# A four-layer cross-attention kernel: q turned by transfers from group 2 on, fused layer-norm rows, and another order in the first pass

## The reference

```
L0: xn = layer_norm(x); q, k, v from xn and context with weights quantised to {-g, 0, g}
    x = x + softmax(q k^T / sqrt(8)) v Wo           16 heads of 8
L1: self-attention, cross-attention (16 heads of 8, masks), feed-forward of 512 with gelu,
    each with residual and layer_norm
L2: vision = mean of context; three steps of routing weights; fused = text + gate * weighted
    out = layer_norm(fused) * gamma + beta
L3: h = rmsnorm(x); q = h Wq (16 heads of 64), k, v = rmsnorm(context) Wk, Wv (4 heads of 64)
    q = q*cos + rotate_half(q)*sin;  k = k*cos + rotate_half(k)*sin
    x = x + softmax(q k^T / 8 + mask) v Wo;  x = x + (silu(h Wgate) * (h Wup)) Wdown
```

## Time and profile before

| | |
|---|---|
| Median of 3 runs | 474.1 us (473.9 to 476.17) |
| The profiled execution | 470.89 us |
| Its span | 469.0 us |
| PE busy | 433.0 us, 92% |
| DVE busy | 372.8 us, 79% |
| ACT busy | 298.4 us, 64% |
| POOL busy | 285.2 us, 61% |

### The profile page before, as it was taken

One profiled execution on the slowest core, in us unless ns is written; L12 is line 12 of the kernel. 1 busy time (PEld: TensorE's weight loads), 2 busy tenths in 40 slices (PEclk: granted clock), 3 DMA queues, 4 the chain that ended last, 5 costly groups with the idle time before them and its releaser, 6 DMA issues.

```text
span 469.0 us, 16877 instructions
## 1 busy us (share of the span) xinstructions
PE 433.0 (92%) x6824; PEld 348.2 (74%) x6824; DVE 372.8 (79%) x927; ACT 298.4 (64%) x726; POOL 285.2 (61%) x323
## 2 busy tenths in 40 slices
PE   5899999999999999999888888989999999989896
PEld 4467777766767777689877666888888888878676
DVE  5598898689999898877788987869788686868553
ACT  1478777678787776766873656566575757654452
POOL 6565733357878787965553666558566666753430
PEclk9999999999999999999999999999999999999999
DMA  8990000000000000000000000000000000000000
GB/s 275 235 288 13 3 2 3 2 3 3 1 4 3 1 4 3 2 1 2 1 1 3 2 1 3 1 13 3 14 3 1 14 3 13 1 14 1 15 1 24
DMA packets 12436, 11.54 MB, mean 25 GB/s; under 512 B 5192, under 2 KB 10312, under 8 KB 12360
## 3 DMA queue, kind: packets, MB, share of 16 engines
q1 hardware_dynamic: 11640, 9.01, 7.4%
q10 hardware_dynamic: 720, 1.45, 0.9%
HBM read 9.42 MB, written 1.05 MB: 22 GB/s over the span
## 4 chain that ended last, share of the span: by engine, by line
PE 50%; DVE 24%; ACT 10%; issue 8%; POOL 7%; DMA 1%; POOLq 0%; ACTq 0%; DVEq 0%
PE ps L471 9%; PE ps L485 6%; PE ps L453 6%; POOL p L1929 4%; PE ps L461 3%; PE ps L639 3%; ACT shared L864 2%; PE ps L411 2%; PE ps L537 2%; PE ps L412 2%; PE ps L501 2%; ACT p L858 2%; PE ps L420 2%; DVE sm L1654 2%; DVE wide L1564 2%
## 5 line engine op out<-in xcount | busy, mean ns | idle before, releaser
L1346 DVE TENSOR_REDUCE negm<-ps 128x8 bf16<-128x512 f32 x96 | 59.6, 683 | 20.8 <-PE ps L453 20.8
L1879 POOL TENSOR_TENSOR wide<-wide,cv 128x1024 f32<-128x1024 f32 x24 | 45.6, 1899 | 44.3 <-ACT wide L848 44.3
L858 ACT ACTIVATE p<-ps 128x512 f32<-128x512 f32 x96 | 57.1, 598 | 23.4 <-PE ps L461 21.9
L864 ACT ACTIVATE shared<-ps 128x512 f32<-128x512 f32 x96 | 55.1, 604 | 20.1 <-PE ps L471 20.1
L471 PE MATMUL ps<-cst,p 128*128 128x128 f32 x384 | 61.2, 282 | 2.6 <-ACT p L858 0.6
L471 PEld LDWEIGHTS ps<-cst,p 128*128 128x128 f32 x384 | 42.2, 141 | 26.0 <-ACT p L858 15.1
L1822 POOL TENSOR_TENSOR rstd<-veps,neghalf 128x2 f32<-128x2 f32 x40 | 28.9, 721 | 41.9 <-DVE veps L1382 23.8
L1929 POOL TENSOR_TENSOR p<-p,mx 128x512 f32<-128x512 f32 x32 | 33.9, 1060 | 29.0 <-DVE mx L1650 28.7
L1936 POOL TENSOR_TENSOR probs<-p,rc 128x512 f32<-128x512 f32 x32 | 33.4, 1054 | 7.9 <-DVE rc L1657 7.8
L1059 ACT ACTIVATE p<-p 128x512 f32<-128x512 f32 x32 | 20.1, 631 | 21.5 <-POOL p L1929 21.5
L461 PE MATMUL ps<-negm,idb 128*128 128x512 bf16 x96 | 32.8, 382 | 0.4 <-DVE negm L1346 0.4
(11 more groups left out here) (214 smaller groups left out, 1131.3 us busy)
## 6 DMA issues: line engine op xcount, KB each, us to landing
m<-in_mask_l SPq DMA_DIRECT2D x2, 512.0 KB, 12.8
result<-x_all SPq DMA_DIRECT2D x7, 128.0 KB, 1.8
x_all<-in_x_tok SPq DMA_DIRECT2D x1, 768.0 KB, 7.0
wide<-in_ctx_t SPq DMA_DIRECT2D x1, 768.0 KB, 8.5
rv<-in_rv ACTq DMA_DIRECT2D x1, 768.0 KB, 8.4
wa<-in_wa SPq DMA_DIRECT2D x1, 512.0 KB, 9.0
w<-in_w SPq DMA_DIRECT2D x2, 256.0 KB, 7.5
wq<-in_wq SPq DMA_DIRECT2D x1, 512.0 KB, 7.7
```

The lines of the kernel that those rows point to most:

```text
L858: A_(p3[:, n % 3, :], ps[:, S_BANK[r], :], ACT.Exp, scale=SC8).then_inc(sm["act_exp"], 1)
L864: A_(pt[:, w % 2, r, :], pt_bank(RG * w + r), ACT.Copy).then_inc(sm["act_pt"], 1)
L1346: V.tensor_reduce(negm[:, n % 4, :], ps[:, S_BANK[r], :].rearrange("p (a k) -> p a k", k=S), AX.X, ALU.max, negate=True).then_inc(sm["dve_ ...
L1879: P.tensor_tensor(r_op[:, w % 2, :, :], k_t[:, w % 2, :].unsqueeze(1).to_broadcast([128, 4, GT]), head_masks.unsqueeze(2).to_broadcast([12 ...
```

## The change

**q turned in full (groups 2 to 7).** VectorE makes q*(-sin) into `q_sin` (in `shared`) with `sine`, and q*cos into `q_rows` with `read_q`: eight operations of 128x512 a group in place of four of 128x1024. SyncE copies `q_sin` to `q_swap` with the halves of 32 partitions exchanged: for each pair of q tiles four transfers of 32 partitions x 4 KB. GpSimd adds `q_swap` to `q_rows` (`turn_q`, four operations of 128x512). The scores are one product with `kt`; `kcs` and the fill `ks` are gone for these groups. The mask is added by VectorE as before.

**Order of the last stage.** q2 and q3 are filled at the end of the first half. VectorE makes q0, q1 at the end of its first half and q2, q3 at the head of its second; `rotate_k` stands ahead of `out`. GpSimd's `turn_q` are in its second half, two between the subtracts and two at the end. ScalarE reads `l_in` ahead of `exps3`.

**Fused rows.** `l2_norm` and `l2_affine` are replaced by `l2_rows` in all rounds.

**Pass 0.** `x` comes in three pieces; the loads that ScalarE issued (`rv`, `cst`) are issued by SyncE; ScalarE normalises groups 0 and 1 and makes two of unit 0's four masked keys; the quantisation's scales take three operations in place of four; unit 1's transposes and projections stand inside unit 0 of TensorE's loop, and ScalarE reads them after unit 0's first exponential.

```diff
         HALVES = (
             (("s0", 0), ("s1", 0), ("pv0", -1), ("pv1", -1), ("l_in", 2), ("md", -2), ("l_text", 2), ("k", 2), ("out", -1),
-             ("in", 1), ("l_gate", 2), ("t0", 0), ("t1", 0), ("q0", 1), ("q1", 1)),
-            (("s0", 0), ("s1", 0), ("pv0", -1), ("pv1", -1), ("m_in", -1), ("kt", 2), ("ks", 2), ("q2", 1), ("q3", 1),
-             ("out", -1), ("v", 2), ("mg0", -1), ("mu0", -1), ("l_back", 2), ("t0", 0), ("mg1", -1), ("mu1", -1), ("t1", 0)),
+             ("in", 1), ("l_gate", 2), ("q0", 1), ("q1", 1), ("t0", 0), ("t1", 0), ("q2", 1), ("q3", 1)),
+            (("s0", 0), ("s1", 0), ("pv0", -1), ("pv1", -1), ("m_in", -1), ("kt", 2),
+             ("v", 2), ("out", -1), ("mg0", -1), ("mu0", -1), ("l_back", 2), ("t0", 0), ("mg1", -1), ("mu1", -1), ("t1", 0)),
         )
...
+            def swap_halves(g):
+                half = HD3 // 2
+                for a in range(2):
+                    eng.wait_ge(sm["q_sin"], 4 * (g - TURNED) + 2 * a + 2)
+                    if g > TURNED:
+                        eng.wait_ge(sm["q_rot"], 4 * (g - TURNED - 1) + 2 * a + 2)
+                    two = slice(2 * a, 2 * a + 2)
+                    for i in range(4):
+                        to, of = half * i, half * (i ^ 1)
+                        eng.dma_start(q_swap[to:to + half, two, :], q_sin[of:of + half, two, :])\
+                           .then_inc(sm[f"q_swap{a}"], 16)
...
+            normalise_in(0)
+            act.wait_ge(sm["ld_small"], 32)
+            A_(idb[:, 0, :], cst[:, 0:128], ACT.Copy).then_inc(sm["cst_bf"], 1)
             evac_in(0)
             evac_qk(0)
+            mask_half()
+            normalise_in(1)
             evac_in(1)
-            evac_qk(1)
...
                 exps(w, 0)
+                if w == 0:
+                    evac_qk(1)
                 exps(w, 1)
...
+            def q_times(g, i, to, c):
+                tab = cst[:, C_ROPEQ + c * S:C_ROPEQ + c * S + S].unsqueeze(1).to_broadcast([128, 2 * GB, S])
+                return V.tensor_tensor(to, bank_of(f"q{i}", g).rearrange("p (b q) -> p b q", q=S), tab, ALU.mult)
...
@@ VectorE, first_half(r)
                 if r < NG - 1:
-                    l2_norm(r + 1)
+                    l2_rows(r + 1)
                 read("mg1", r - 2)
                 read("mu1", r - 2)
...
                     sum3(2 * n + 1)
+                if r + 2 < NG:
+                    rotate_k(r + 2)
                 if 1 <= r < NG:
                     read("out", n - 1)
                     m_rms_mean(r - 1)
                 if r + 2 < NG:
                     l2_max(r + 2)
+                if r + 1 < NG:
+                    sine(r + 1, 0)
+                    read("q0", r + 1)
+                    read("q1", r + 1)
                 if r + 2 < NG:
-                    rotate_k(r + 2)
                     l2_gate(r + 2)
...
@@ GpSimd
+            def turn_q(g, i):
+                pool.wait_ge(sm[f"q_swap{i // 2}"], 64 * (g - TURNED + 1))
+                pool.wait_ge(*released(f"q{i}", g))
+                P.tensor_tensor(q_rows(g, i), q_rows(g, i), q_swap[:, i, :].rearrange("p (b q) -> p b q", q=S), ALU.add)\
+                    .then_inc(sm["q_rot"], 1)
...
@@ GpSimd, second_half(r)
+                if r + 1 < NG:
+                    turn_q(r + 1, 0)
                 if r < NG:
                     subtract3(4 * r + 2)
+                if r + 1 < NG:
+                    turn_q(r + 1, 1)
+                if r < NG:
                     subtract3(4 * r + 3)
                 if r + 2 < NG:
                     l2_fuse(r + 2)
                 if r < NG:
                     probs3(4 * r + 2)
                     probs3(4 * r + 3)
+                if r + 1 < NG:
+                    turn_q(r + 1, 2)
+                    turn_q(r + 1, 3)
```

More of the change, by code:

```diff
@@ L265, in build @@
         SECOND = (
-            (("s0", 0), ("s1", 0), ("l_back", 1), ("pv0", -1), ("pv1", -1), ("l_in", 2), ("kt", 1), ("ks", 1), ("k", 2),
-             ("l_text", 2), ("out", -1), ("l_gate", 2), ("t0", 0), ("in", 1), ("t1", 0), ("q0", 1), ("q1", 1)),
+            (("s0", 0), ("s1", 0), ("l_back", 1), ("pv0", -1), ("pv1", -1), ("l_in", 2), ("kt", 1), ("k", 2),
+             ("l_text", 2), ("out", -1), ("l_gate", 2), ("t0", 0), ("in", 1), ("q0", 1), ("q1", 1), ("t1", 0), ("q2", 1), ("q3", 1)),
             HALVES[1],
@@ L744, in scores3 @@
                 for a in range(2):
-                    if u == 0 and a == 0:
-                        pe.wait_ge(*released("q1", g))
+                    if u == 0 and g >= TURNED:
+                        pe.wait_ge(*released("kt", g))
+                        pe.wait_ge(sm["q_rot"], 4 * (g - TURNED) + 2 * a + 2)
+                    elif u == 0:
+                        pe.wait_ge(*released(("q1", "q3")[a], g))
                         pe.wait_ge(*released("ks", g))
-                    if u == 0 and a == 1:
-                        pe.wait_ge(*released("q3", g))
-                    for c in range(2):
+                    for c in range(1 if g >= TURNED else 2):
+                        q, k = (q3_turned[gs][:, a], k3[:, g % KEPT, 0, a]) if g >= TURNED else \
+                            (q3[gs][a][:, c], k3[:, g % KEPT, c, a])
                         for i in range(2):
@@ L1106, in joining @@
                 read("kt", 2)
-                read("ks", 2)
                 exps3(5)
@@ L1173, in second_half @@
                 if r + 2 < NG:
-                    read("ks", r + 2)
                     read("v", r + 2)
@@ L1294, in quantise @@
                 V.tensor_tensor(w, w, pos, ALU.add).then_inc(sm["quant"], 1)
-            def norm0(g):
-                dve.wait_ge(sm["ln0_r"], g + 1)
-                for t in range(TG):
-                    ins = V.tensor_scalar(xn_all[:, TG * g + t, :], x_all[:, TG * g + t, :], mv[:, g % 2, t, 0:1],
-                                          rstd[:, g % 2, t:t + 1], ALU.subtract, ALU.mult)
-                ins.then_inc(sm["ln0"], 1)
             def halves():
@@ L1524, in l2_stats @@
                 layer_norm(lambda t: fused[:, g % 2, t * 128:t * 128 + 128], g, "g_", g % 2, st2, mv2, veps2)
-            def l2_norm(g):
-                gs = g % 2
-                dve.wait_ge(sm["g_r"], g + 1)
-                if g >= 2:
-                    dve.wait_ge(sm["g_x"], g - 1)
-                for t in range(TG):
-                    ins = V.tensor_scalar(yn2[:, gs, t, :], fused[:, gs, t * 128:t * 128 + 128], mv2[:, gs, t, 0:1],
-                                          rstd2[:, gs, t:t + 1], ALU.subtract, ALU.mult)
-                ins.then_inc(sm["g_yn"], 1)
             def l2_rows(g):
@@ L1556, in m_rms_mean, with sine @@
                     .then_inc(sm["m_ms"], 1)
+            def q_times(g, i, to, c):
+                tab = cst[:, C_ROPEQ + c * S:C_ROPEQ + c * S + S].unsqueeze(1).to_broadcast([128, 2 * GB, S])
+                return V.tensor_tensor(to, bank_of(f"q{i}", g).rearrange("p (b q) -> p b q", q=S), tab, ALU.mult)
+            def sine(g, a):
+                if g > TURNED:
+                    dve.wait_ge(sm[f"q_swap{a}"], 64 * (g - TURNED))
+                for i in range(2 * a, 2 * a + 2):
+                    dve.wait_ge(sm["p_use"], filled(f"q{i}", g))
+                    q_times(g, i, q_sin[:, i, :].rearrange("p (b q) -> p b q", q=S), 1).then_inc(sm["q_sin"], 1)
             def read_q(g, i):
-                if g >= 2 and i == 0:
-                    dve.wait_ge(sm["s3"], TG * (g - 1))
+                if g >= TURNED:
+                    if i == 0:
+                        dve.wait_ge(sm["s3"], TG * (g - 1))
+                    return q_times(g, i, q_rows(g, i), 0)
                 tab = cst[:, C_ROPEQ:C_ROPEQ + 2 * S].rearrange("p (c q) -> p c q", c=2).unsqueeze(2)\
@@ L1688, in joining @@
                 sum3(5)
+                rotate_k(3)
                 read("out", 1)
@@ L1691, in joining @@
                 l2_max(3)
-                rotate_k(3)
+                sine(2, 0)
+                read("q0", 2)
+                read("q1", 2)
                 l2_gate(3)
@@ L1725, in second_half @@
                 if r + 1 < NG:
-                    read("q0", r + 1)
-                    read("q1", r + 1)
+                    sine(r + 1, 1)
+                    read("q2", r + 1)
+                    read("q3", r + 1)
                 if live:
```

133 lines of the change are left out of this document (76 added, 57 removed).

## The result

The changed kernel takes 496.8 us in the median (495.66 to 498.51, 4 runs), the kernel before on the same chip 474.0 (472.59 to 476.17). The ratio is 1.050, with a 95% interval from 1.046 to 1.054: 5% slower. The forecast was 491 us, in a range of 472 to 501. The profiled execution took 497.29 us.

A forecast was written before the change was run, and what follows sets the result against it. Two limits were taken to overlap: TensorE's total and a dependence loop through the softmax on VectorE and GpSimd. 5 x 2.1 + 4 x 1.8 + 0.9 - 1.0 - 0.5 = +17 gave 491 us, range 472 to 501.

The forecast's parts named there:

- R to M: Last stage, mask-add of second token block (R) to next group's first (M): GpSimd's queue delays `pow`; +2.1 in five rounds.
- Late transfers: Rival: q's exchange transfers land late and delay GpSimd's subtract by 3.3 us, five times: 507 us; chance 0.13.
- M to R: Last stage, a group's first mask-add (M) to its second block's (R): VectorE's `rotate_k` and eight q passes; +1.8, four rounds.
- Joining: The round before the steady ones: loses two halves of `sum_k(2)`, gets the same reorder; 0, between -2 and +2.
- Start: Start of the kernel: the second unit's transposes and scores come earlier; -0.5 us, between -2.5 and +0.5.
- Last pair: Last two halves, with no group behind: 22.66 us becomes 23.6, +0.9.
- TensorE sets the round: Rival: added GpSimd and VectorE work sits in idle time, each of five rounds falls by up to 3.3: 456 us; chance 0.13.
- The sums find gaps: Rival: both interval terms come out near nothing, the round stays about 26: 473.5 us, or 471; chance 0.12.

The follow-up runs named there:

- the edit: Changed kernel with the previous pass 0, `rotate_k` behind `out`, q2's and q3's sums on VectorE, plus `rotate_k(3)` behind `out` and its mean in the joining: 482.76 us.
- old start: Changed kernel with pass 0 and the loads as in the kernel before: 493.94 us, ratio 1.044 to the kernel before.
- `pow`: Changed kernel with GpSimd's power of the layer-norm statistics moved ahead of q3's sum, behind q2's: 494.71 us, ratio 1.048 to the kernel before.
- `rotate_k`: Changed kernel with VectorE's rotation of k moved behind the read of `out`, ahead of the mean: 490.91 us, ratio 1.038 to the kernel before.
- no exchange: Changed kernel without the 48 transfers; GpSimd adds the sine product with halves not exchanged: 495.17 us, ratio 1.048 to the kernel before.
- rows unfused: Changed kernel with `l2_norm` and `l2_affine` put back in place of `l2_rows`: 493.64 us, ratio 1.044 to the kernel before.

## Why the prediction was right, and where it was not

- **R to M, +2.1 forecast.** Right in mechanism and size: +1.8 to +1.95 in three rounds. The `pow` began at R + 10.8 (forecast 11.0), VectorE waited 2.26 (2), the fused rows took 1.26 (1.25). The forecast took R from the chain (373.58), which shows this instruction 0.07 later than the timeline; that moves 0.07 between the two intervals. Both parts were taken apart: the fused rows are 0.68 a round in the kernel before, and with q2's and q3's sums moved from ahead of the `pow` to VectorE's wait 1.05 to 1.2 a round goes. The first theory of how to get it back (the `pow` one place ahead) failed on contention.
- **Late transfers (the rival with 0.13).** Right in one round of five for 1.4 us and in another for 0.6, not in all five. From the first issue (358.81) to the first sum were 4.2 us, where the forecast had 3.1 and a cover of 4.5: an issue takes 0.59 in the median (forecast 0.43) and a landing 2.3 (1.8). That it mostly fitted was a margin of 0.3, and luck. The Trainium skill (DMA: Bandwidth & Descriptors, section Rules for kernel authors) says that transfers to disjoint halves of the partitions serialise, and by that page's fit 512 KB gave an estimate of 3.2; the trace is 1.0 above it, and no run here tells whether the four serialise on the engines or only follow their issues.
- **M to R, +1.8 forecast, +1.13 measured.** The path is right and its pieces are a little too long. Measured, with the forecast in brackets: `rotate_k` starts at M + 6.57 (`kk` ready at 6.53), `l2_max` is done at M + 10.13 (10.45), the gate takes 0.36 (0.71), the eight passes 4.79 (4.88): 15.28 in place of 16.0. The sentence that `l_in` "counts for nothing" is wrong of the kernel before, where moving it alone gives 0.95 a round. It didn't enter the sum: the forecast's path starts at `kk`, which is ready at M + 6.5 with and without the move. Against a kernel that has the move (13.20), the rest of the change costs 2.08: 0.86 for `rotate_k`, and by difference about 1.2 for the q passes.
- **Joining, 0 forecast, +4.9 measured.** Failed, and the largest error. I set "the same reorder" against the two halves of `sum_k(2)` that go, and walked neither ScalarE's queue nor TensorE's fills here. About 2.5 of it is `rotate_k` ahead of `out`, as the edit showed, and 1.35 is eight fills at the low clock (3.32 in place of 1.97); the rest is open. The traces differ by 26.5 us and the forecast's sum was 17.1; of the 9.4 that were missed, 3.6 is the chance of the two executions. Of the rest the joining is the most. The other misses have both signs (M to R came out 2.7 under its forecast, the last pair 2.1 over) and cancel in part, which is luck.
- **Start, -0.5 forecast.** The changed kernel's trace shows +2.6, the runs of the start alone -0.6 to +2.4, in which both the forecast and a cost of 1 or 2 us lie.
- **Last pair, +0.9 forecast, +3.0 in the trace.** Its first half took 14.75 there and 13.06 or 13.07 in five variants that hardly touch this part (old start, `pow`, `rotate_k`, no exchange, rows unfused); the clock was 0.58 between 444 and 448 us. The whole pair took 25.62 there and 23.92 to 24.54 in the five, so 1.1 to 1.7 of the +3.0 is that one execution's, and +1.3 to +1.9 stays, against +0.9.
- **TensorE sets the round (0.13).** Not so in the changed kernel. But with `l_in` moved TensorE is full in the kernel before, with a round of 25.5 us. There a saving of 2.6 on TensorE may be worth something, if VectorE and GpSimd are given nothing for it; no run tested that.
- **The sums find gaps (0.12).** Not so: in the third round GpSimd had no gap from 363.00 to the `pow`, and neither interval kept its length.

## What to carry to other kernels

Where an engine is at 97% in a round and still stalls once, follow what comes behind the stall before calling it slack; removing that one stall (one move) gave 1%, while the change that took work off the full engine and gave it to its neighbours, with its reorders, cost 5%. Price an addition to an in-order queue by what stands behind it, in each different round, also in those that occur once: the steady rounds' price said nothing on the joining. A transfer that just fits is a bound for every later improvement. And before the difference of two intervals is put down to an edit, compare how long the same matmuls took in both.

## What the runs showed of the hardware

TensorE's granted clock falls after its stalls, and not always after the same ones. Ahead of the last stage it stands 1.47 and then 0.66 us in the kernel before and after alike; the sixteen q fills behind take 3.69 us at clock 1.00 in the one (start 243.85), and 5.38 in the other. These are the latter's row and its clock (1.00 is 2.4 GHz, 0.50 is 1.2 GHz):

```profile
246.44 5.38 PE L659 MATMUL ps<-shared,wq 128*128 128x256 f32 x16 [0.66 <-ACT shared L1070]
```
```profile
240.00:256.00 16.00, 13.88 (x195) 0.89 0.00 1
```

The kernel before with fused rows lost the same 1.5 us there, with that code untouched; in all, seven of the 14 traces lost it. In the start, traces with the same code differ by up to 2.0. So single traces can differ by 1.5 to 3.5 us with the same code in these places, and a difference of that size needs the runs. Slow matmuls cost time only on the path: in four of the changed kernel's five rounds the second eight of line 697 took 2.80 to 3.32 in place of 1.89, yet R to M was 14.04, 14.20 and 14.14 with 3.32, 1.89 and 2.80. In the joining, where VectorE waits for the fills, they cost their whole 1.6.

Contention between VectorE and GpSimd showed as 1.62 for 0.61 (a pair of fused rows), 2.44 for 0.75 (a pair of k's sine products, 289.12 above, beside GpSimd's products of the probabilities), and 1.10 for 0.71 on GpSimd's side (the `pow` beside VectorE's sums).
